# A perceiver block's point-cloud stage: part of the norm statistics from VectorE to ScalarE, part of a subtraction from GpSimd to VectorE

## The reference, cut

```python
def _get_graph_features(feats, inds_list, perm, W_lin, b_lin, k=K):      # K = 10, 4 orders, B, N, C = 2, 1024, 64
    ...
    x16 = x.astype(jnp.float16).astype(jnp.float32)
    qh = x16.reshape(B * N, k, nheads, headdim)                          # 8 heads of 64
    scores = jnp.einsum('bihd,bjhd->bhij', qh, qh) / np.float32(np.sqrt(headdim))
    attn = jax.nn.softmax(scores, axis=-1)
    out = jnp.einsum('bhij,bjhd->bihd', attn, qh).reshape(B * N, k, total)
    fused = out @ W_lin.T + b_lin
    return fused.reshape(B, N, k, 128)
...
h1 = jnp.einsum('oc,bnkc->bonk', W_conv1, g1)
h1 = _lrelu(_instance_norm(h1, (2, 3)))       # mean and variance over all points and windows of a batch
feats1 = h1.max(axis=-1)
```

## Time and profile before

| | |
|---|---|
| median of 3 runs | 995.19 us (989.38 to 995.51) |
| the profiled execution | 993.34 us, of which 991.7 us is the span from first to last instruction |
| PE, DVE, ACT, POOL busy over the span | 922.2, 733.9, 392.1, 452.0 us |
| point cloud, layer 1: first to last `normalise` | 502.49 to 667.96 us |
| point cloud, layer 2: first to last `normalise` | 718.17 to 894.30 us |

### The profile page before, as it was taken

One profiled execution on the slowest core, in us unless ns is written; L12 is line 12 of the kernel. 1 busy time (PEld: TensorE's weight loads), 2 busy tenths in 40 slices (PEclk: granted clock), 3 DMA queues, 4 the chain that ended last, 5 costly groups with the idle time before them and its releaser, 6 DMA issues. The chain is left out here.

```text
span 991.7 us, 36771 instructions
## 1 busy us (share of the span) xinstructions
PE 922.2 (93%) x15278; PEld 701.0 (71%) x15279; DVE 733.9 (74%) x1931; ACT 392.1 (40%) x679; POOL 452.0 (46%) x410
## 2 busy tenths in 40 slices
PE   4899899999999999999978988879989999999998
PEld 2799879696969687765965666657955656665695
DVE  7698738866657483897967989886879999997410
ACT  6343414141433323212354555554355555553010
POOL 1101212531211202020299999980499999986000
PEclk9999999999999999999998999999979999999999
DMA  9998797888878796566257666672357665662650
GB/s 365 407 408 308 259 337 261 294 304 295 312 273 308 258 353 224 188 260 255 93 89 128 130 141 134 134 138 63 109 104 126 127 127 125 126 128 46 262 247 22
DMA packets 148961, 204.95 MB, mean 207 GB/s; under 512 B 99409, under 2 KB 101137, under 8 KB 148498
## 3 DMA queue, kind: packets, MB, share of 16 engines
q1 hardware_dynamic: 55058, 172.06, 48.9%
q10 hardware_dynamic: 91392, 23.34, 14.2%
q0 software_dynamic: 2432, 8.42, 2.4%
HBM read 154.45 MB, written 1.61 MB: 157 GB/s over the span
## 5 line engine op out<-in xcount | busy, mean ns | idle before, releaser
L546 PEld LDWEIGHTS ps<-hT,ring 128*128 128x128 f32 x2304 | 258.1, 192 | 6.7 <-issue 5.7
L546 PE MATMUL ps<-hT,ring 128*128 128x128 f32 x2304 | 260.0, 275 | 0.8 <-ACT xc L692 0.8
L1614 PE MATMUL ps<-PT,ring 128*64 128x120 f16 x2752 | 100.0, 225 | 27.8 <-ACT OT L1774 14.1
L1782 ACT CAST PP<-S 128x480 f16<-128x480 f32 x86 | 66.9, 778 | 125.4 <-POOL S L2043 125.4
L1614 PEld LDWEIGHTS ps<-PT,ring 128*64 128x64 f16 x2752 | 87.0, 113 | 37.8 <-issue 27.4
L978 POOL TENSOR_TENSOR y_y<-y_z,sgate 128x512 f32<-128x512 f32 x16 | 20.1, 1272 | 193.0 <-DVE y_z L909 193.0
L579 PE MATMUL ps<-wt,y_n 128*128 128x512 f32 x224 | 99.4, 596 | 1.4 <-DVE xs L901 1.4
L2050 POOL TENSOR_TENSOR PP<-S,PP 128x480 f16<-128x480 f32 x86 | 97.9, 1139 | 5.7 <-ACT PP L1782 5.7
L2043 POOL TENSOR_TENSOR S<-S,den 128x480 f32<-128x480 f32 x86 | 86.7, 1008 | 16.9 <-DVE den L1916 15.8
L808 DVE SCALAR_TENSOR_TENSOR xc<-xpad,parg,xc 128x128 f32<-128x128 f32 x192 | 59.3, 372 | 42.2 <-ACT xc L692 41.0
L1774 ACT COPY OT<-ps 128x960 f32<-128x960 f32 x86 | 81.2, 944 | 12.5 <-PE ps L1614 12.5
(11 more groups left out here) (328 smaller groups left out, 1478.6 us busy)
## 6 DMA issues: line engine op xcount, KB each, us to landing
ring<-in_w_in SPq DMA_DIRECT2D x36, 2048.0 KB, 9.3
wt<-in_w_out SPq DMA_DIRECT2D x14, 2048.0 KB, 7.8
PT<-P_turned SPq DMA_DIRECT2D x332, 64.0 KB
ring<-in_w SPq DMA_DIRECT2D x8, 1024.0 KB, 12.9
ctx_chunks<-in_ctx SPq DMA_DIRECT2D x4, 1024.0 KB, 8.8
krow<-keys_scratch POOLq DMA_DIRECT2D x8, 512.0 KB, 7.5
mchunk<-in_mask_t POOLq DMA_DIRECT2D x8, 512.0 KB, 8.7
ring<-in_w_out SPq DMA_DIRECT2D x2, 2048.0 KB, 8.0
```

The source lines that it names most:

```text
L546: mm = nc.tensor.matmul(ps[:, bank, j * T:(j + 1) * T], weights[:, j, kc * P:(kc + 1) * P], k.hT[:, kc, :], start=kc == 0, stop=kc == KC - 1)
L1614: mm = nc.tensor.matmul(ps[half, out_bank(it) + slot // 4, at:at + 4 * ROWS], XR[:, slot, half], PT[:, :, r * SLOTS + slot, 0:ROWS, part], ...
L1782: sc.copy(c.PP[ph % 2][:, :, 0:ROWS, 0], c.S[ph % 2][:, :, :]).then_inc(s_hi, 1)
```

## The change

Two edits, and the waits that go with them.

1. Of one batch (`own`: layer 1's only `bn_stats`, layer 2's second) the steps 1 to 37 are no longer read by `bn_stats`. Instead ScalarE's new `moments` (lag 6, behind `turn_rows` in its stream) passes H twice, with the first step's mean subtracted as a bias: once as it is, once squared, each with a sum along the row as second output; the elements themselves go to PSUM banks that nobody reads. TensorE's `linear` now also waits for `moments` of the step that last used its bank. `first_moments` (VectorE, once a layer) makes the first step's mean; `early_statistics` makes mean and variance out of the sums.
2. In layer 1 `low_part` on GpSimd makes 11 of the 16 slots. The other 5 are made by VectorE's new `low_share` (lag 1), which stands between `shift` and `turn`. Its two inputs, `S` and the f16 part in `PP`, both lie in SBUF.

```diff
@@
 EARLY = STEPS - 5
+SPENT_BANK, MOMENT_LAG = (2, 7), 6
+LOW_SHARE = (11, 2 * SLOTS)
@@
+        own = nb - 1
+        moments0 = (layer - 1) * (EARLY - 1)
+        summed = lambda it: not isinstance(it, int) or 1 <= it < EARLY
@@
                     return
                 if after(it, 2):
                     pe.wait_ge(s_red, t0 + it - 1)
+                    if summed(it - 2):
+                        pe.wait_ge(c.s_moments, moments0 + it - 2)
@@
+            def moments(it, ph):
+                if not inside(it) or not summed(it):
+                    return
+                act.wait_ge(s_red, t0 + it + 1)
+                if isinstance(it, int) and it == 1:
+                    act.wait_ge(s_part, part0 + 3)
+                H = ps[:, H_BANK + ph % 2, own * COLS:(own + 1) * COLS]
+                at = c.stats[:, own, it, :] if isinstance(it, int) else c.stats[:, own, bass.ds(it, 1), :].rearrange("p a s -> p (a s)")
+                spent = [ps[:, SPENT_BANK[ph % 2], i * COLS:(i + 1) * COLS] for i in range(2)]
+                sc.activation(spent[0], H, ACT.Identity, bias=c.mean_off[:, 0:1], accum_out=at[:, 0:1])
+                sc.activation(spent[1], H, ACT.Square, bias=c.mean_off[:, 0:1], accum_out=at[:, 1:2]).then_inc(c.s_moments, 1)
             def step(it, lagged):
                 high_part(*lagged(1))
                 exponentials(*lagged(0))
                 unload(*lagged(PV_LAG))
                 turn_rows(*lagged(0))
+                moments(*lagged(MOMENT_LAG))
@@
                 raw = c.f1[:, None, :] if layer == 1 else c.f2[:, :, :]
                 H = ps[:, H_BANK + ph % 2, 0:nb * COLS].rearrange("p (b n) -> p b n", b=nb)
                 for b in range(nb):
+                    if b == own and summed(it):
+                        continue
                     st = c.stats[:, b, it, :] if isinstance(it, int) else c.stats[:, b, bass.ds(it, 1), :].rearrange("p a s -> p (a s)")
                     vec.bn_stats(st, H[:, b, 0:cols])
                 win = H.rearrange("p b (n j) -> p b n j", j=WIN)
@@
+            def low_share(it, ph):
+                if layer == 2 or not inside(it):
+                    return
+                v.wait_ge(s_hi, t0 + it + 1)
+                own_slots, PP = slice(*LOW_SHARE), c.PP[ph % 2]
+                vec.tensor_tensor(PP[:, own_slots, 0:ROWS, 1], c.S[ph % 2][:, own_slots, :], PP[:, own_slots, 0:ROWS, 0], ALU.subtract).then_inc(c.s_lo_share, 1)
             def turn(it, ph):
                 if not inside(it):
                     return
                 v.wait_ge(s_lo, t0 + it + 1)
+                if layer == 1:
+                    v.wait_ge(c.s_lo_share, t0 + it + 1)
@@
             def step(it, lagged):
                 reduce(*lagged(REDUCE_LAG))
                 shift(*lagged(0))
+                low_share(*lagged(1))
                 turn(*lagged(TURN_LAG))
                 denominators(*lagged(0))
+                if isinstance(it, int) and it == REDUCE_LAG:
+                    first_moments()
                 if isinstance(it, int) and it > STEPS:
                     early_statistics(it)
+            made = [part0]
+            def link(ins):
+                made[0] += 1
+                ins.then_inc(s_part, 1)
+                return made[0]
+            def first_moments():
+                v.wait_ge(s_red, t0 + 1)
+                v.wait_ge(s_part, link(vec.bn_aggr(c.first[:, :], c.stats[:, own, 0, :])))
+                link(vec.tensor_scalar(c.mean_off[:, :], c.first[:, 0:1], -1.0, None, ALU.mult))
+                link(vec.tensor_scalar(c.first[:, 1:2], c.first[:, 1:2], float(COLS), None, ALU.mult))
             def early_statistics(it):
+                early = lambda b: c.stats[:, b, EARLY - 1, :]
+                count = float(EARLY * COLS)
                 if it == STEPS + 2:
                     v.wait_ge(s_red, t0 + EARLY)
-                    for b in range(nb):
-                        vec.bn_aggr(c.partial[:, b, :], c.stats[:, b, 0:EARLY, :].rearrange("p s w -> p (s w)")).then_inc(s_part, 1)
+                    v.wait_ge(c.s_moments, moments0 + EARLY - 1)
+                    total = link(vec.tensor_reduce(c.sums[:, :], c.stats[:, own, 1:EARLY, 0:2].rearrange("p s w -> p w s"), AX, ALU.add))
+                    for b in range(own):
+                        link(vec.bn_aggr(c.partial[:, b, :], c.stats[:, b, 0:EARLY, :].rearrange("p s w -> p (s w)")))
+                    v.wait_ge(s_part, total)
+                    link(vec.tensor_scalar(c.partial[:, own, 0:1], c.sums[:, 0:1], 1.0 / count, None, ALU.mult))
                 if it == STEPS + 3:
-                    v.wait_ge(s_part, part0 + nb)
-                    for b in range(nb):
-                        early = c.stats[:, b, EARLY - 1, :]
-                        vec.memset(early[:, 3:4], float(EARLY * COLS)).then_inc(s_part, 1)
-                        vec.tensor_copy(early[:, 4:5], c.partial[:, b, 0:1]).then_inc(s_part, 1)
-                        vec.tensor_scalar(early[:, 5:6], c.partial[:, b, 1:2], float(EARLY * COLS), None, ALU.mult).then_inc(s_part, 1)
+                    v.wait_ge(s_part, made[0])
+                    square = link(vec.tensor_tensor(c.sums[:, 0:1], c.sums[:, 0:1], c.partial[:, own, 0:1], ALU.mult))
+                    link(vec.memset(early(own)[:, 3:4], count))
+                    link(vec.tensor_tensor(early(own)[:, 4:5], c.partial[:, own, 0:1], c.mean_off[:, :], ALU.subtract))
+                    for b in range(own):
+                        link(vec.memset(early(b)[:, 3:4], count))
+                        link(vec.tensor_copy(early(b)[:, 4:5], c.partial[:, b, 0:1]))
+                        link(vec.tensor_scalar(early(b)[:, 5:6], c.partial[:, b, 1:2], count, None, ALU.mult))
+                    v.wait_ge(s_part, square)
+                    link(vec.scalar_tensor_tensor(out=early(own)[:, 5:6], in0=c.sums[:, 1:2], scalar=c.first[:, 1:2], in1=c.sums[:, 0:1],
+                                                  op0=ALU.add, op1=ALU.subtract))
             walk(v, step)
             v.wait_ge(s_red, t0 + STEPS)
-            v.wait_ge(s_part, part0 + 4 * nb)
+            v.wait_ge(s_part, made[0])
@@
                     return
                 PP = c.PP[ph % 2]
                 pool.wait_ge(s_hi, t0 + it + 1)
-                gp.tensor_tensor(PP[:, :, 0:ROWS, 1], c.S[ph % 2][:, :, :], PP[:, :, 0:ROWS, 0], ALU.subtract).then_inc(s_lo, 1)
+                mine = slice(0, LOW_SHARE[0] if layer == 1 else 2 * SLOTS)
+                gp.tensor_tensor(PP[:, mine, 0:ROWS, 1], c.S[ph % 2][:, mine, :], PP[:, mine, 0:ROWS, 0], ALU.subtract).then_inc(s_lo, 1)
```

More of the change, by code:

```diff
@@ L1362, in __init__ @@
         self.X_more = [k.hT[:, 4 * u:4 * u + 4, :].bitcast(F16) for u in range(PHASES - len(made.X))]
-        self.X, self.X_zeros = made.X + self.X_more, k.sem("c_X_zeros")
+        self.X = made.X + self.X_more
         self.conv_d, self.blocks, self.f16, self.WC = made.conv_d, made.blocks, made.f16, made.WC
@@ L1391, in __init__ @@
         self.partial = sb('early_mean_variance', [P, B, 2])
+        self.first, self.sums, self.mean_off = sb("first_mean_variance", [P, 2]), sb("moment_sums", [P, 2]), sb("minus_first_mean", [P, 1])
+        self.s_moments, self.s_lo_share = k.sem("c_moments"), k.sem("c_P_low_share")
         self.mvb, self.stdb, self.rsb, self.shift, self.cb = sb("mvb", [P, B, 2]), sb("stdb", [P, B]), sb("rsb", [P, B]), sb("shift", [P, B]), sb("cb", [P, 1])
@@ L1452, in stage_cloud_layer @@
         s_end, s_std, s_part, s_soon = sem("end"), *c.layer_sems
-        std0, part0, soon0 = ((layer - 1) * i for i in (1, 4, 16 * B * NHEAD))
+        std0, part0, soon0 = ((layer - 1) * i for i in (1, 9, 16 * B * NHEAD))
         s_bias, s_scaled = c.end_sems
@@ L1461, in stage_cloud_layer @@
             s_early = sem("early_products")
-            s_conv, s_ost, s_ostd, s_ox = (sem(i) for i in ("last_convolution", "out_statistics", "out_std", "out_x"))
+            s_conv, s_ost, s_ox = (sem(i) for i in ("last_convolution", "out_statistics", "out_x"))
             res = c.fsg[:, 0:NT // 2, :].rearrange("p t d -> p (t d)")
@@ L1820, in _ @@
                 act.wait_ge(s_ost, 3)
-                sc.activation(c.o_std[:, :], c.o_mv[:, :][:, 1:2], ACT.Sqrt, bias=k.eps[:, 0:1]).then_inc(s_ostd, 1)
+                sc.activation(c.o_std[:, :], c.o_mv[:, :][:, 1:2], ACT.Sqrt, bias=k.eps[:, 0:1]).then_inc(s_std, 1)
                 act.wait_ge(s_bias, bias0 + 2)
@@ L1970, in _ @@
                 vec.bn_aggr(c.o_mv[:, :], c.o_stats[:, :, :]).then_inc(s_ost, 1)
-                v.wait_ge(s_ostd, 1)
+                v.wait_ge(s_std, std0 + nb + 1)
                 vec.reciprocal(c.o_rs[:, :], c.o_std[:, :]).then_inc(s_ost, 1)
@@ L1993, in _ @@
                 for more in c.X_more:
-                    gp.memset(more, 0.0).then_inc(c.X_zeros, 1)
+                    gp.memset(more, 0.0).then_inc(k.cloud.filled, 1)
                 pool.wait_ge(k.PT_zeros, 32)
```

(2 more changed lines are left out.)

## The result

The changed kernel takes 1020.78 us (median of 4, 1016.88 to 1022.72), the kernel before 994.39 (median of 4). The ratio is 1.0266, 95% interval 1.0236 to 1.0295: slower by 26.4 us, where 30.8 had been summed up. The profiled execution took 1020.02 us, with a span of 1018.4.

A forecast was written before the change was run, and what follows sets the result against it. GpSimd was taken to bound layer 1, PE layer 2. The terms 21.1 + 5.3 + 1.5 + 0 + 2.9 = 30.8 us on 993.34 gave 1024.1, forecast as 1025 us, range 1012 to 1036, chance 0.80.

The forecast's parts named there:

- The bound and the mechanism: Layer 1: GpSimd sets the pace; low_share, with two SBUF inputs, waits for the end of GpSimd's differences in every step.
- The rival that the engines do not exclude each other: Layer 1: low_share takes about 0.25 us inside differences, step 3.80, 992 to 996 us, no change; chance 0.08.
- the rival that GpSimd's saving arrives: Layer 1: low_share's chain does not bind, 0.33 x 39 = -13 us, about 984, faster; chance 0.04.
- The step: Layer 1's loop: a step grows from 3.866 to 4.62 us, +21.1 us over 28 steps (+19.7 to +23.1).
- The first eleven steps: Start of layer 1, 502.5 to 548.0: other waits fit into the longer step, +5.3 us; +8.3 if it comes on top.
- The last three steps: End of layer 1 and drain: turn stands behind a part waiting for a later cast, +1.5 us, estimate 0.5 to 3.
- The end of layer 2: Small instructions with two SBUF tensors wait for GpSimd's L2065, bn_aggr starts later: +2.9 us, 1.5 to 3.5.
- Layer 2's loop and the sums on ScalarE: Dropped bn_stats give 0 (-5 to +0.5); moments, 1.2 us a pair, is covered by ScalarE's wait, 0.
- 2.3 would have made it the bound: Rival, layer 2: moments takes 2.3 us a pair, ScalarE's step of 4.5 passes PE's 4.2, 1036 us; chance 0.02.
- The clock: Rival, layer 1: PE's share falls to 73%, the clock drops for half the loop, +10 us, 1035; chance 0.06.
- The 13 cases of the prediction: Mixer of the kernel before: in 13 of 13, VectorE instructions with two SBUF inputs ended just after the GpSimd instruction.

The follow-up runs named there:

- e3: Changed kernel, but ScalarE first copies S of the five slots to PSUM and low_share reads it there: 1001.75 us, ratio 1.0056 to the kernel before.
- e4: Changed kernel with one slot (30 columns) on VectorE instead of five (150): 1016.42 us, ratio 1.0175 to the kernel before.
- e7: Changed kernel with GpSimd's differences in layer 1 as two instructions of half the size: 999.0 us, ratio 1.0061 to the kernel before.
- e9: Changed kernel with low_share as two instructions (two slots, then three), same inputs: 1049.63 us, ratio 1.0562 to the kernel before.
- e1: Changed kernel without low_share: GpSimd makes all 16 slots, the two ScalarE sums stay; 998.04 us, ratio 1.0013 to the kernel before.
- e5: As e1, with three small instructions at layer 2's end as tensor_scalar, one SBUF tensor and one-column pointers: 992.45 us, ratio 0.999 to the kernel before.
- e8: Kernel before plus low_share reading S from PSUM, its five slots cast and copied first, other casts behind the exponentials; bn_stats kept: 992.38 us, ratio 0.9986.

## Why the prediction came true, by its steps

**The bound and the mechanism held.** GpSimd set the pace of layer 1, and the instruction meant to relieve it waits for it: e3 takes the wait away by moving one operand, e4 shows that the columns hardly matter, e7 that a shorter GpSimd instruction ends it sooner, e9 that each further instruction can wait anew. The rival that the engines do not exclude each other is out; its step of 3.80 is near what e3 shows once the hold is gone (3.93, with the copy in the chain). So is the rival that GpSimd's saving arrives: GpSimd waits for `den` instead, 0.83 us in the step shown, where 1.1 was foreseen. The saving itself is there: `low_part` takes 1.16 us in the earlier trace rows and 0.84 where nothing holds it (e3, e9), 0.32 less, as forecast. In the changed kernel it takes 0.91, being held by `low_share` in its turn, and it no longer overlaps the next `normalise`, which in the earlier trace rows it does by 0.09 (608.77 + 1.16 against 609.84); by these two the idle time is shorter.

**The step was 0.10 too long.** Forecast 4.62, measured 4.52: +18.4 us in 28 steps instead of 21.1, just below the lower end of 19.7. The place is the stretch from `den` to the reciprocal. I took 0.69 from the earlier trace rows, where `den` starts after idle time; directly behind `turn` it is 608.93 - 608.30 = 0.63. The rest is 0.04 at the end of `differences`: 607.57 - 604.75 = 2.82 from the start of `normalise`, where 2.86 was taken.

**The first eleven steps** cost 49.97 - 45.5 = +4.5 against +5.3 taken: nearly 11 x 4.52 = 49.7. The other waits were absorbed, as chosen, but for one step of 5.32; that the sum comes so near is in part luck, since the first step took only 3.93.

**The last three steps** cost nothing: 681.6 to 693.3 is 11.7 us, as before, instead of +1.5. The drain behind them, from the last `normalise` to `bn_aggr`, took 13.52 us against 12.60, but it takes 13.42 and 15.06 in e1 and e5, which have no `low_share`, so nothing shows that the 0.9 is its doing. The 1.5 was an estimate without a row of its own.

**The end of layer 2** cost +2.98 (+2.9), and e5 shows that the two inputs are the cause.

**Layer 2's loop and the sums on ScalarE** were put at nothing. PE's share is the same. The pair takes 0.99 us where 1.2 was taken and 2.3 would have made it the bound, and it lies in ScalarE's wait, though in layer 2 only just: the wait was 1.3 us in the earlier trace rows, and in 784 to 900 us now it is 5.8 / 27 = 0.2.

```profile
ACT PP L1792 <- POOL S L2108: 5.8, 27, 0.3
```

From first to last `normalise` layer 2 took 172.8 us in this profile, 3.3 less than before; but over all profiles here that stretch lies between 172.8 and 178.9 (the highest in e8, which has no sums), and most of the scatter falls into its first eleven steps. In the 28 steps of the loop the eight profiles with the sums lie at 116.6 to 116.9 us and the three without at 117.2 to 117.7; between the two kernels' own profiles it is 117.2 to 116.6, so some 0.6 us is the sums'.

**The sum** of what was measured is 18.4 + 4.5 + 0 + 3.0 - 0.6 = 25.3, the medians differ by 26.4. The start of layer 1 alone moves between 502.5 and 505.0 us from profile to profile, so a difference of a microsecond has no further cause that could be named.

**The clock** stayed at 1.00 in the loop, although PE's share there fell to 95.13 / 126.63 = 75%. In the first steps it was at the lower of its two levels for some 17 us, longer than in the earlier trace rows, behind 7.7 us in which PE had been busy 4.99:

```profile
509.00:516.70 7.70, 4.99 (x202) 4.16 (x200) 6.31 (x10) 3.74 (x11) 6.88 (x6) 1.00 0.57 87
517.00:533.50 16.50, 13.73 (x326) 9.31 (x324) 13.76 (x28) 7.73 (x13) 13.21 (x12) 0.50 0.70 114
```

The steps in it took 4.52 us like the others, except that of 5.32 at its end, so it cost at most 0.8 us. That rival is out for this kernel.

The Trainium skill (*SBUF — State Buffer*, section *Who interferes with whom*) says that a VectorE instruction with at most one SBUF input, outside the modes that use both of its ports, does not contend with GpSimd, and that one with two contends with a GpSimd instruction that reads SBUF, not with one that only writes it. The runs agree on the inputs: 0.346 us with one input, 1.16 with two. On GpSimd's side the mixer of the kernel before agrees too. The 13 cases of the prediction all stand beside GpSimd instructions that read tensors in SBUF, as `differences` does; beside GpSimd's memsets, which only write, an instruction with two inputs from SBUF (L808) was not held:

```profile
L1316 POOL MEMSET X<- x2: 971/972/972, 172.6 to 173.5; 128x1024 f16 x2
L1316 POOL MEMSET PP<- x2: 971/971/971, 174.4 to 175.3; 128x1024 f16 x2
L808 DVE SCALAR_TENSOR_TENSOR xc<-xpad,parg,xc x10: 345/348/352, 173.0 to 175.5; 128x128 f32<-128x128 f32 x10
L808 DVE SCALAR_TENSOR_TENSOR xc<-xpad,parg,xc x4: 340/340/1589, 208.8 to 210.9; 128x128 f32<-128x128 f32 x4
```

The 1589 ns in the last row are those of the one that started at 208.82, beside L961 of the earlier trace rows.

## What to carry to other kernels

Before work goes from GpSimd to VectorE, look where each operand lies: with two tensors in SBUF the instruction waited in these runs for the end of the GpSimd instruction that was reading SBUF, however small it was itself, and everything behind it in VectorE's stream waited too. A copy of one operand to PSUM on an engine with time to spare (0.3 us here) or a per-partition pointer in place of a one-column tensor took that wait away here. In the profile such a wait looks like work: compare the duration of an instruction with the same one elsewhere, and its end with GpSimd's.

## What was not expected of the hardware

The size of the instruction does not protect it: one column lasted 5.46 us. Two instructions of VectorE in a row did not go through together: GpSimd's next instruction came in between (e9). And GpSimd pays as well when VectorE comes first: in e7 the two halves take 2.17 us with `low_share` between them, 2.02 without it (547.31), and the whole 1.88, so about 0.14 us is the second start and 0.15 the hold by `low_share`.
